# Graph layers on one core: the second adjacency product with whole units in single precision

## The reference

```
h = relu(layernorm(x))
z = leaky_relu(d * (adj @ (d * h)) @ W1 + b1)        # d = 1/sqrt(row sums of adj)
S = exp(-sqrt(|z_i - z_j|^2 + 1e-10) / 2), kept only at the 4 largest of each row
x = x + d2 * ((S + adj) @ (d2 * h)) @ W2 + b2        # d2 = 1/sqrt(row sums of S + adj)
h = relu(layernorm(x))
out = x + h @ W_self.T + (adj @ h) @ W_neigh.T + b
```

## Time and profile before

| | |
|---|---|
| median of three runs | 1301.8 us |
| profiled execution | 1301.95 us, span 1300.3 us |
| TensorE busy | 938.8 us, 72% |
| VectorE busy | 867.5 us, 67% |
| GpSimd busy | 661.7 us, 51% |
| ScalarE busy | 597.6 us, 46% |
| mean granted TensorE clock | 0.886 of full |

### The profile page before, as it was taken

The page is one execution under the profiler, slowest core; times in us unless marked ns, Lnnn a source line. Parts: engine busy times, 40 slices in busy tenths (PEclk is TensorE's granted clock), DMA queues, the critical chain, the costliest instruction groups (busy, mean ns, idle before and its releaser), DMA issues.

```text
span 1300.3 us, 13534 instructions
## 1 busy us (share of the span) xinstructions
PE 938.8 (72%) x3570; PEld 665.8 (51%) x3570; DVE 867.5 (67%) x843; ACT 597.6 (46%) x1105; POOL 661.7 (51%) x937
## 2 busy tenths in 40 slices
PE   0133163465668899899999994577777777799998
PEld 0111031232233444477777773455666666588886
DVE  0955474455444321279999999947777777788785
ACT  0533342354442321255555555535555554567673
POOL 9798877877830000044444444588888887200000
PEclk9975676886888899899999998798888888899999
DMA  9999999999998874295444445695777777599993
GB/s 222 323 348 370 361 346 366 360 365 366 345 363 319 307 255 171 73 269 210 157 155 155 158 156 203 186 385 209 276 284 270 280 275 273 216 362 381 378 378 127
DMA packets 115653, 357.73 MB, mean 275 GB/s; under 512 B 34464, under 2 KB 59808, under 8 KB 87456
## 3 DMA queue, kind: packets, MB, share of 16 engines
q1 hardware_dynamic: 59296, 273.11, 55.1%
q0 software_dynamic: 47104, 80.00, 20.6%
q10 hardware_dynamic: 9216, 4.20, 1.2%
HBM read 250.02 MB, written 106.95 MB: 275 GB/s over the span
## 4 chain that ended last, share of the span: by engine, by line
PE 40%; POOL 19%; DMA 19%; issue 10%; DVE 7%; ACT 2%; SPq 1%; POOLq 0%; ACTq 0%; DVEq 0%
DMA araw<-in_adj_dram 16%; POOL zt_lo L567 11%; PE ps L1138 7%; POOL araw L350 7%; PE ps L1227 5%; PE ps L1230 5%; PE ps L1228 5%; PE ps L1229 5%; PE ps L1250 4%; PE ps L1251 4%; PE ps L1252 4%; DVE part L872 2%; DVE tr L857 1%; DMA hw_scratch<-z_st 1%; DMA xs<-in_x_dram 1%
## 5 line engine op out<-in xcount | busy, mean ns | idle before, releaser
L350 POOL DMA_DIRECT2D araw<-in_adj_dram x512 | 302.2, 599 | 65.6 <-ACTq L628 25.2
L999 DVE TENSOR_TENSOR araw_r<-araw,tr_r 128x2048 fp32r<-128x2048 f32 x128 | 289.8, 2297 | 45.9 <-ACT tr_r L722 45.5
L722 ACT ACTIVATE tr_r<-araw 128x2048 fp32r<-128x2048 f32 x128 | 241.8, 1911 | 67.4 <-PE ps L1252 41.5
L567 POOL DMA_INDIRECT zt_lo<-neighbour_table,idx_st x128 | 197.2, 1541 | 45.7 <-issue 40.0
L705 ACT ACTIVATE araw<-ps,nsq 128x1024 f32<-128x1024 f32 x128 | 142.8, 1117 | 113.3 <-PE ps L1230 90.7
L1250 PE MATMUL ps<-araw_r,zt_hi 128*128 128x512 f32 x256 | 110.9, 433 | 90.1 <-issue 33.7
L624 ACT ACTIVATE ps<-araw 128x256 f32<-128x256 f32 x304 | 111.4, 367 | 65.0 <-DMA araw<-in_adj_dram 61.5
L872 DVE TENSOR_REDUCE part<-araw 128x16 f32<-128x4096 f32 x13 | 57.4, 4414 | 97.4 <-DMA araw<-in_adj_dram 97.4
L1227 PE MATMUL ps<-sq_rows,pick 128*128 128x512 f32 x256 | 102.2, 399 | 17.1 <-ACT araw L705 9.5
L1250 PE MATMUL ps<-araw_r,ys_r 128*128 128x512 f32 x256 | 101.7, 397 | 9.3 <-DVE araw_r L999 9.3
L1250 PEld LDWEIGHTS ps<-araw_r,zt_hi 128*128 128x128 f32 x256 | 52.6, 205 | 106.6 <-issue 65.5
(11 more groups left out here) (150 smaller groups left out, 1632.6 us busy)
## 6 DMA issues: line engine op xcount, KB each, us to landing
araw<-transposed SPq DMA_DIRECT2D x156, 1024.0 KB, 5.1
araw<-in_adj_dram POOLq DMA_DIRECT2D x512, 128.0 KB, 20.7
keys_scratch<-araw SPq DMA_DIRECT2D x64, 512.0 KB, 4.3
transposed<-tr SPq DMA_DIRECT2D x28, 1024.0 KB, 8.2
transposed<-unit_zt_hi SPq DMA_DIRECT2D x12, 1024.0 KB, 9.1
transposed<-unit_zt_lo SPq DMA_DIRECT2D x12, 1024.0 KB, 9.8
transposed<-unit_sq_rows SPq DMA_DIRECT2D x12, 1024.0 KB, 9.4
xs<-in_x_dram SPq DMA_DIRECT2D x64, 64.0 KB, 2.0
```

The lines of the kernel that those rows point to most:

```text
L350: gp.dma_start(araw[R * q + first:R * q + R:SPREAD, c], adj_v[q, first:R:SPREAD, g // 2, g % 2, :, c]).then_inc(a_first_in[c], DMA)
L567: gp.indirect_dma_start(out=gath[:, i, u, k, :], out_offset=None, in_=table, in_offset=bass.IndirectOffsetOnAxis(ap=idx_st[:, i, u * TOPK ...
L722: act.activation(ring_hi[:, place % TSLOTS], ring[:, j], ACT.Copy).then_inc(hi_done, 1)
L999: v.tensor_tensor(ring_lo[:, j], ring[:, j], ring_hi[:, place % TSLOTS].bitcast(F32), ALU.subtract).then_inc(lo_done, 1)
```

## The change

The second product multiplies whole units in single precision, by the unsplit scaled features; no unit and no feature is split for it. `split_high` and `split_low` remain for the third product. The rounded copy of the new features moves from GpSimd to ScalarE (behind the normalisation), their low part to VectorE (`keep_low`, behind the residual of the group before). The bias b is added on TensorE, by a matmul of a row of ones with the bias row, into the same sums as W_self. GpSimd only gathers. The table is made in two halves, set between the scaled features of units 0, 1 and 2, and lies in `zt_lo` instead of `hs`; the rounded new features lie in `zt_hi` and `sq_rows`. The loops of the second and third product on ScalarE and VectorE are written out; those on TensorE, GpSimd and SP stay loops.

```diff
+            def whole_unit(g2, j, bank):
+                pe.wait_ge(a_in[j], g2 * DMA + (B_IN[j] + DMA))
+                for i in range(U):
+                    ins = pe.matmul(acc[bank], ys[:, i * GROUPS + j], ring[:, j, i], start=j == 0 and i == 0, stop=j == GROUPS - 1 and i == U - 1)
+                ins.then_inc(u_used, 1)
...
             def finish_second_c(g):
                 pe.wait_ge(zt_ev, g + (GROUPS + 1))
                 pe.wait_ge(q_done, g + GROUPS)
-                four(ps_q, flat(t_st[:]), ws_t[:]).then_inc(q_mm, 1)
+                for u in range(U):
+                    pe.matmul(ps_q[:, u * F:u * F + F], t_st[:, u], ws_t[:], start=True, stop=False)
+                    ins = pe.matmul(ps_q[:, u * F:u * F + F], neghalf[0:1], bias[0:1], start=False, stop=True)
+                ins.then_inc(q_mm, 1)
...
                     if isinstance(g, int) and g == 0:
-                        pe.wait_ge(y_lo_done, j + 1)
-                    unit(g, j, i, y_hi, y_lo)
+                        pe.wait_ge(y_ready, GROUPS + j + 1)
+                    whole_unit(g, j, i)
...
+            second_y(0)
             v.wait_ge(hw_in, QD * DMA)
+            table_part(0, TILES // 2)
+            second_y(1)
+            table_part(TILES // 2, TILES).then_inc(gw_ready, 1)
+            for g in range(2, GROUPS):
+                second_y(g)
...
             with gp.Fori(1, GROUPS // 2) as pair:
                 for i in range(2):
-                    keep_h2(pair * 2 + (i - 2))
                     gather_group(pair * 2 + i, i)
-            for i in range(2):
-                keep_h2(GROUPS - 2 + i)
...
                 ins.then_inc(h2_done, 1)
+                act.wait_ge(h2_done, g + 1)
+                act.activation(hi_g[:, g], z_st[:], ACT.Copy).then_inc(h_hi_done, 1)
...
+            def keep_low(g):
+                v.wait_ge(h_hi_done, g + 1)
+                v.tensor_tensor(lo_g[:, g], z_st[:], hi_g[:, g].bitcast(F32), ALU.subtract).then_inc(kept, 1)
...
+            for g in range(GROUPS - 1):
+                finish_second_a(g)
+                finish_second_b(g)
+                if g >= 1:
+                    finish_second_c(g - 1)
+                keep_low(g)
```

More of the change, by code:

```diff
@@ L714, in _ @@
                     leave(pair * 2 + par, par, pair)
[L716 to L725, removed]
             vals_f = vals[:].rearrange("p t k -> p (t k)")
@@ L732, in _, with split_high, evacuate @@
             act.activation(tmp32[:], tmp32[:], ACT.Sqrt).then_inc(deg2_root, 1)
[L734 to L742, removed]
+            def split_high(g2, j):
+                place = g2 * GROUPS + j - UNITS
+                if place >= TSLOTS:
+                    act.wait_ge(u_used, UNITS + place - TSLOTS + 1)
+                act.wait_ge(a_in[j], g2 * DMA + B_IN[j] + DMA)
+                act.activation(ring_hi[:, place % TSLOTS], ring[:, j], ACT.Copy).then_inc(hi_done, 1)
+            def evacuate(g, bank, used, turn):
+                act.wait_ge(u_used, used)
+                act.wait_ge(z_mm, turn)
+                act.wait_ge(z_done, turn)
                 act.activation(out_t_m, by_block(acc[bank]), ACT.Copy).then_inc(acc_read, 1)
@@ L780, in _ @@
-            act.wait_ge(gw_ready, 1)
-            group_second(0, 0, first=2)
-            group_second(1, 1, prev=0)
-            with act.Fori(1, GROUPS // 2) as pair:
-                for i in range(2):
-                    group_second(pair * 2 + i, i, prev=pair * 2 + (i - 1), before=pair * 2 + (i - 2))
-            for place in range(GROUPS):
-                split_high(GROUPS, place)
-                if place == 2:
-                    evacuate(GROUPS - 1, 1, 0, GROUPS)
-                if place == 3:
-                    transposed_second(GROUPS - 2)
-                    spread_second(GROUPS - 1)
-                    normalize_second(GROUPS - 1)
@@ L1090, in group_third @@
+            for g in range(GROUPS):
                 for j in range(GROUPS):
                     split_low(g + GROUPS, j)
-                    if j == 2 and isinstance(g, int):
-                        finish_second_c(GROUPS - 1)
-                    if j == 3:
-                        finish_third(prev, 1 - i)
-            group_second(0, 0, None, None, first=2)
-            group_second(1, 1, 0, None)
-            with v.Fori(1, GROUPS // 2) as pair:
-                for i in range(2):
-                    group_second(pair * 2 + i, i, pair * 2 + (i - 1), pair * 2 + (i - 2))
@@ L1297, in _ @@
             pe.wait_ge(wt_ev, 2)
+            pe.wait_ge(ones_ready, 1)
+            pe.wait_ge(bias_in, 3 * DMA)
             group_second(0, 0, None, None)
```

194 lines of the change are left out of this document (78 added, 116 removed).

## The result

The changed kernel took 1302.05 us (median of 20 runs, 1295.69 to 1309.2), the kernel before 1308.85 (20 runs): a ratio of 0.9952, 95% interval 0.9936 to 0.9968. It is faster by half a per cent where 3.3 were forecast. The profiled execution took 1297.09 us, span 1295.4; held against the 1259.6 forecast for it, 37.5 us are missing.

A forecast was written before the change was run, and what follows sets the result against it. It took gathers to pace the second product and TensorE the third. Savings of 11.7 (start), 29.6 (groups) and 1.0 (boundary) sum to 42.3 us: 1301.95 to 1259.6, stated as 1259, range 1250 to 1276.

The forecast's parts named there:

- the three rivals: Gathers keep their length (1278 us, chance 0.07), loads of units become the bound (1279, 0.05), slower clock (1314, 0.06).
- The start: Start of the second product: TensorE begins at 814.6 instead of 826.26, 11.7 us earlier.
- The gathers: GpSimd in the second product: gathers near 1.0 us instead of 1541 ns, 22.1 us per group; VectorE waits for one once.
- The rival that gathers keep their length: Second product: their own queue stretches gathers, GpSimd stays at 30.5 us per group; 1278 us, chance 0.07.
- What bounded the kernel before: Second product before the change: gathers on GpSimd, not the matmuls, pace its groups of 33.9 us.
- The loads: Rival in the second product: unit loads become the bound at 33.4 us per group; 1279 us, chance 0.05.
- The whole units: TensorE in the second product: eight units in full single precision take 27.45 us per group.
- The bias matmuls: TensorE in the second product: four over one partition charged 0.89 us per group, as four small products; bounds 0 and 1.78.
- each change of weights paid in full: Upper bound for the second product's bias matmuls: 1.78 us per group, twice the four small ones.
- Groups on the clock: Second product: groups from 814.6, 844.9, 873.2, then six of 30.56 us, ending at 1056.6; 242.0 us instead of 271.6.
- The boundary: Second product's end to the third product's fifth unit: 21.5 us instead of 22.5, with TensorE standing 3.2 and 4.3.
- The slow clock: Rival in the second product: full-precision matmuls without rest get the lower clock; +55 us, 1314; chance 0.06 with similar causes.

The follow-up runs named there:

- e1: The changed kernel with TensorE's loop over groups 2 to 7 of the second product written out; 1305.99 us, ratio 0.9975 to the kernel before.
- f3: The changed kernel issuing 4 of the 16 gathers of each group, the first neighbour's rows standing in for the other three; 1283.71 us, a single run.
- e4: The changed kernel with the bias matmuls over all 128 partitions (ones in row 0, zeros below); 1295.22 us, a single run.
- f1: The changed kernel with GpSimd starting the gathers of group g only when 8g units are used; 1278.35 us, ratio 0.9781 to the kernel before.
- f4: The changed kernel reloading only half of each unit in groups 1 to 7 of the second product, output wrong; 1278.29 us, a single run.
- h3: f4 again (half reloads in groups 1 to 7), on the chip of h1; 1276.59 us.
- h1: The changed kernel word for word, on another chip; 1279.84 us, ratio 0.98 to the kernel before.
- e2: The changed kernel with the bias added by VectorE instead of four matmuls over one partition on TensorE; 1282.05 us, ratio 0.9782 to the kernel before.
- f2: The changed kernel with f1's waits before gathers and e2's bias on VectorE; 1256.1 us, ratio 0.9623 to the kernel before.
- e3: The changed kernel with both e1's written-out TensorE loop and e2's bias on VectorE; 1284.92 us, ratio 0.9806 to the kernel before.
- g4: e2 again (the changed kernel with the bias on VectorE), on the chip of g1; 1283.44 us, a single run.
- h4: The changed kernel with h2's held gathers and e2's bias on VectorE; 1259.75 us, ratio 0.9642 to the kernel before.
- g3: The changed kernel with f1's waits in GpSimd's program put on a semaphore long satisfied, so nothing is spaced; 1301.34 us, ratio 0.9957 to the kernel before.
- h2: The changed kernel with gathers of groups 1, 2 and 3 held until 11, 18 and 26 units are used; 1278.02 us, ratio 0.9789 to the kernel before.
- i2: h2 again (gathers of groups 1 to 3 held), on one more chip; 1297.5 us, ratio 0.9898 to the kernel before.
- g2: f1 again (gathers of group g wait for 8g used units), on the chip of g1; 1282.36 us, ratio 0.9807 to the kernel before.
- g1: The changed kernel again, word for word, on another chip; 1298.62 us, ratio 0.9942 to the kernel before.

## Why the prediction was wrong

The time lies outside the range 1250 to 1276, and what happened is none of the three rivals: no gather kept its length, no unit waited for a load, and full-precision matmuls kept the full clock.

**The start: right in kind, 1.5 us late.** Forecast 814.6, measured 816.09 (first scaled features at 815.23). Among the executions of this study the first whole unit started anywhere from 813.68 (e1) to 823.03 (f3), with the code ahead of it unchanged but for a memset in e4; so this term can't be judged closer than some microseconds.

**The gathers: right.** 1018 ns against "near 1.0"; the one wait of VectorE for them is there (859.43 in place of 858). The rival that gathers keep their length fell: beside whole units, with no subtraction of a unit running, none takes 2.27. And where such a subtraction came back, so did the long gathers: in f1 the last three of the last group, beside low parts from 1062.70 on, took 3.10, 1.90 and 1.90 us, those ahead of them 1.01 to 1.14. The Trainium skill, page "SBUF — State Buffer", section "Who interferes with whom", reports that a two-input operation did not stall the issue of DMAs; for these indirect DMAs the traces don't agree.

**What bounded the kernel before: misread, without effect on the sum.** The prediction says that the gathers paced the second product. In its steady groups (904 to 1090) VectorE never waited for a gather. TensorE stood once per group, when it had used up the low parts made ahead:

```profile
919.92 0.79 PE L1250 MATMUL ps<-araw_r,zt_hi 128*128 128x512 f32 x1 [6.76 <-issue]
```

The low part that it lacked was begun at 917.57 and done at 919.86, behind VectorE's 8.1 us of closing. Gathers took about as long per group as this chain, but nothing shows that anyone waited for them. The change removes both, so the forecast came out the same.

**The loads: right to give them little.** No whole unit waits for a load, and half loads save little or nothing (f4 1278.29 against f1's 1278.35, h3 1276.59 against h1's 1279.84).

**The whole units: right.** e2's group of 29.69 less its small products (0.89 + 0.44 + 0.89) leaves 27.47 for eight, against 27.45. With the bias off TensorE, f2's second product runs from 813.90 to 1049.33, 235.4 us; the prediction's 242.0 less six times 0.89 is 236.7.

**The bias matmuls: a term mis-sized.** Charged 0.89 per group, bounded at 1.78; measured 3.22 - 0.89 = 2.33 in the row, and 32.12 - 29.69 = 2.43 between groups with and without them (e2), above the upper bound. "Nearest are the four small ones" holds for matmuls of one depth (e4: 0.89, as charged), not for these, which alternate between 128 partitions and one; and the bound "each change of weights paid in full" left out what one partition costs between full ones. Against e4's group it is 6 x (32.12 - 30.59) = 9.2 us over the forecast. In two groups the clock fell behind them as well (33.82 instead of 32.12): 3.4 more. This belongs to them too: all thirteen executions with bias matmuls over one partition have one to four such groups, and the six without them (e2, e3, e4, f2, g4, h4) none.

**Groups on the clock: the step that failed.** It let TensorE run from unit to unit with nothing but its own work. At the start of group 2 it lost 22.2 us in which no load and no semaphore held it and instructions simply did not come. Nothing in the rows of before showed it. There the gathers of the first two groups also ran without a pause, for 60.3 us (839.86 to 900.20), and TensorE, after a rest of 18.29 us for VectorE, worked at full pace through their end (6.00 of 6 us and 32 records from 894 to 900); none of SyncE's register instructions took longer than 0.22 us. Which chip that was isn't known. Together 22.2 + 9.2 + 3.4 = 34.8; the second product took 276.5 us (816.09 to 1092.60) instead of 242.0, 34.5 more.

**The boundary: right in sum.** 21.3 us against 21.5. TensorE stood 1.17 and 2.28 instead of 3.2 and 4.3, because it had more to do between (the bias matmuls, and a unit at the lower clock). After the fifth unit 181.5 us follow, 180.0 before: 1.5 worse than the 0 that was taken. There the last group's small products stand, 3.22 us until 1130.15 against 0.80 before; the prediction charged no bias matmuls for them. Sum: 1.5 + 34.5 - 0.2 + 1.5 = 37.3 of 37.5.

**The slow clock: a rival that fell.** Full-precision matmuls hold 1.00 for whole groups (1.00 from 1000 to 1032). The low clock of the stretch (0.55 from 876 to 906) comes after the gaps, not before them: the first records between gaps still last 0.59 us, in e1 three of them, and only the later ones 1.01.

What the runs show of the stretch: it comes on some chips (three of five, and in the first result) and not on others. There SyncE's instructions can be late beside short runs of gathers too; TensorE and ScalarE were caught only late in a run of 43 us or more, from 31 to 41 us after its first gather, and this ends when GpSimd pauses. Breaking the run shortens or moves the loss; the length of GpSimd's program (g3) and TensorE's loop (e1) are no part of it. Open is the mechanism, why one chip has it and another, with runs of 65 to 110 us, does not, and whether full DMA engines are needed, since f3, f4 and h3 ran on chips that show no late instruction. Holding the gathers of all groups was not tried on a chip that has it, alone or with e2's edit.

## What to carry to other kernels

Before believing a cure, run the sick kernel beside it on the same chip: f1 to f4 all looked like cures. When the engine that issues gathers is set free, look at how long it now works without a rest; a pause that costs nothing (h2 against h1) was worth 10 to 16 us on the two chips with the stretch where it was tried (waits on `u_used`: i2, g2). And don't put a matmul over one partition between full ones on the engine that sets the pace: add the bias on an idle engine (15 to 22 us between kernels of one chip: g1 and g4, h2 and h4, f1 and f2), or give it full depth.

## What the runs showed that was not expected

- On three of five chips TensorE, VectorE, ScalarE and SyncE got their instructions late beside a long run of GpSimd's gathers: matmuls 1.4 to 2.1 us apart, a ScalarE evacuation 13.57 us late. The Trainium skill, page "SBUF — State Buffer", section "Who interferes with whom", says that TensorE and ScalarE never wait on anyone; of data ports that may be so, and these runs show only that their instructions did wait, while gathers ran.
- A register instruction of SyncE tells the two kinds of chip apart: 0.04 us always on the two without the stretch, up to 1.42 us beside gathers on the others.
- The same program differs by 27 us (1279.84 and 1307.03) between two chips on which the kernel before differs by 4 (1305.68 and 1309.63).
- Eight matmuls of 128 columns take 1.78 us if all are 128 partitions deep, and 3.22 if every second one is one partition deep. The duration of a weight load is the same for both; it starts with its matmul instead of ahead of it.
